# Local attention: per-head exponentials on ScalarE that take the maximum as bias and accumulate the denominators

## What is computed

```python
def local_attention(q, k, v):
    b, h, n, d = q.shape                       # 2, 8, 1024, 64
    w = n // WINDOW                            # windows of 64
    bq = q.reshape(b, h, w, WINDOW, d) * QK_SCALE
    ...
    bk, bv = (look_around(bk), look_around(bv))          # the window before and this one
    ...
    sim = jnp.einsum('bhwid,bhwjd->bhwij', bq, bk)
    mask = (i < j) | (i > j + WINDOW) | (j == -1)
    sim = jnp.where(mask, -jnp.finfo(sim.dtype).max, sim)
    attn = jax.nn.softmax(sim, axis=-1)
    out = jnp.einsum('bhwij,bhwjd->bhwid', attn, bv)
    return out.reshape(b, h, n, d)
```

## Time and profile before

| | us |
|---|---|
| median of 3 runs | 1153.07 (1151.7 to 1158.17) |
| the profiled execution | 1154.28 |
| its span, first to last instruction | 1152.5 |
| mean granted TensorE clock | 0.973 of full |

### The profile page before, as it was taken

One profiled execution on the slowest core, in us unless ns is written; L12 is line 12 of the kernel. 1 busy time (PEld: TensorE's weight loads), 2 busy tenths in 40 slices (PEclk: granted clock), 3 DMA queues, 4 the chain that ended last, 5 costly groups with the idle time before them and its releaser, 6 DMA issues. The chain is left out here.

```text
span 1152.5 us, 22995 instructions
## 1 busy us (share of the span) xinstructions
PE 1072.7 (93%) x8352; PEld 666.0 (58%) x8352; DVE 828.5 (72%) x1522; ACT 633.2 (55%) x1000; POOL 750.5 (65%) x511
## 2 busy tenths in 40 slices
PE   6884899999999999999999999779999898999988
PEld 4552455455454554445545555747777695777677
DVE  6994666666666666666666663579998689888867
ACT  2442356666665565655656564036666455666554
POOL 3662465767677676867667778389986337666526
PEclk8996799999999999999999999889999999999999
DMA  8899621533315243142242100101111100111111
GB/s 257 270 267 354 159 48 48 110 75 83 75 47 111 52 87 89 49 102 59 60 100 65 48 11 20 56 10 31 33 37 37 26 2 15 36 32 33 33 26 36
DMA packets 83456, 89.03 MB, mean 77 GB/s; under 512 B 32740, under 2 KB 66064, under 8 KB 83344
## 3 DMA queue, kind: packets, MB, share of 16 engines
q1 hardware_dynamic: 83344, 87.55, 29.5%
HBM read 53.57 MB, written 24.25 MB: 68 GB/s over the span
## 5 line engine op out<-in xcount | busy, mean ns | idle before, releaser
L863 DVE CUSTOM_DVE_ANT_0 junk<-psum,alibi 128x1024 bf16<-128x1024 f32 x256 | 313.2, 1223 | 205.1 <-PE psum L918 196.8
L834 ACT ACTIVATE E<-psum,keybias_sb 128x1024 f32<-128x1024 f32 x256 | 274.9, 1113 | 234.7 <-PE psum L942 221.4
L767 POOL TENSOR_TENSOR sum_p<-sum_p,E 128x1024 f32<-128x1024 f32 x96 | 232.4, 2421 | 96.2 <-ACT E L834 91.8
L954 PE MATMUL psum<-E,V 128*64 128x512 f32 x1024 | 248.7, 606 | 0.0
L918 PE MATMUL psum<-KH,QH 64*128 64x512 f32 x512 | 118.6, 459 | 12.0 <-PEq L275 6.9
L954 PEld LDWEIGHTS psum<-E,V 128*64 128x64 f32 x1024 | 62.2, 136 | 112.2 <-issue 98.3
L773 POOL TENSOR_TENSOR sum_p<-sum_p,xpos_sb 128x1024 f32<-128x1024 f32 x32 | 76.2, 2382 | 69.0 <-DVE xpos_sb L873 69.0
L918 PEld LDWEIGHTS psum<-KH,QH 64*128 64x128 f32 x512 | 49.4, 189 | 121.5 <-DVE M L863 84.6
L942 PE MATMUL psum<-QH,KH 64*128 64x512 f32 x512 | 102.8, 397 | 5.9 <-DMA QM<-mrow 3.9
L942 PE MATMUL psum<-QL,KH 64*128 64x512 f32 x512 | 101.6, 392 | 0.0
L942 PE MATMUL psum<-QH,KL 64*128 64x512 f32 x512 | 101.4, 392 | 0.0
(11 more groups left out here) (148 smaller groups left out, 2072.5 us busy)
## 6 DMA issues: line engine op xcount, KB each, us to landing
QH<-qa_scratch SPq DMA_DIRECT2D x64, 256.0 KB, 4.2
qa_scratch<-tH SPq DMA_DIRECT2D x8, 1024.0 KB, 5.6
qa_scratch<-tL SPq DMA_DIRECT2D x8, 1024.0 KB, 7.9
QL<-qa_scratch SPq DMA_DIRECT2D x64, 128.0 KB, 4.2
XF<-inverse_scratch SPq DMA_DIRECT2D x32, 256.0 KB, 3.4
vp_att<-v_att SPq DMA_DIRECT2D x64, 128.0 KB, 2.3
KH<-k_scratch SPq DMA_DIRECT2D x16, 256.0 KB, 4.0
KL<-k_scratch SPq DMA_DIRECT2D x16, 256.0 KB, 5.3
```

Of the source, the lines that this page charges most:

```text
L767: pool.tensor_tensor(sum_p[:, s, :], first, E[:, k % 4, :], ALU.add)\
L834: act.activation(E[:, k % 4, :], scores(k % 2), ACT.Exp, bias=kb).then_inc(exp_done, 1)
L863: dve.tensor_tensor_reduce(junk[:, :], banks(max_bank(i, k), 2), alibi[:, s, :], -1.0, BIG, ALU.add, ALU.min, M[:, s, k:k + 1]).then_inc(m ...
L954: last = pe.matmul(banks(6 + i % 2)[HD * ch:HD * ch + HD, :], V[:, g, k, :], E[:, k % 4, ch * 512:(ch + 1) * 512], start=(k == 0), stop=(k ...
```

## The change

`shift_scores` is gone, and `ident_r` with it. `exponentials` becomes eight ACTIVATEs, one per head, of 128 columns each; the bias is that head's column of `nmax` (the negated maximum, now in fp32), and each also writes the sum of its 128 results into its column of `den`. It waits for the maxima. Each of the eight counts on `exp_done`, so all waits for it are in eighths of a tile. `turn_e` waits for four exponentials ahead of the first four transposes and for the other four ahead of the last four. `denominators` keeps the reciprocal alone.

```diff
-    nmax = sb("nmax_att", [P, 2, FH], F32R)
+    nmax = sb("nmax_att", [P, 2, FH])
...
         def exponentials(t, s):
-            need(act, shifted, t + 1)
+            need(act, max_done, t + 1)
             need(act, e_turned, 2 * (t - 1))
-            need(act, den_done, t - 1)
-            act.activation(E[:, s].rearrange("p h c -> p (h c)"), banks(5, 2), ACT.Exp).then_inc(exp_done, 1)
+            need(act, inv_done, t - 1)
+            for n in range(FH):
+                act.activation(E[:, s, n, :], banks(5, 2)[:, n * P:(n + 1) * P], ACT.Exp,
+                               bias=nmax[:, s, n:n + 1],
+                               accum_out=den[:, s, n:n + 1]).then_inc(exp_done, 1)
...
         def maxima(t, s):
             need(dve, scores_done, t + 1)
-            need(dve, shifted, t - 1)
+            need(dve, exp_done, FH * (t - 1))
...
         def denominators(t, s):
-            need(dve, exp_done, t + 1)
-            need(dve, inv_done, t - 1)
-            dve.tensor_reduce(den[:, s, :], E[:, s, :, :], AX_X, ALU.add).then_inc(den_done, 1)
-            need(dve, den_done, t + 1)
+            need(dve, exp_done, FH * (t + 1))
             need(dve, o_done, t - 1)
             dve.reciprocal(den_inv[:, s, :], den[:, s, :]).then_inc(inv_done, 1)
...
         def multiply_qk(t, s):
             need(pe, qkT_done, 2 * (t + 1))
-            need(pe, exp_done, t)
+            need(pe, exp_done, FH * t)
...
-        def shift_scores(t, s):
-
-            need(pe, max_done, t + 1)
-            for n in range(2):
-                last = pe.matmul(banks(5 + n).rearrange("p (h c) -> p h c", c=P), ident_r[:, :],
-                                 nmax[:, s, 4 * n:4 * n + 4][:, :, None].to_broadcast([P, FH // 2, P]),
-                                 start=False, stop=True, skip_group_check=True)
-            last.then_inc(shifted, 1)
-
...
         def turn_e(t, s):
-            need(pe, exp_done, t + 1)
             need(pe, qkT_done, 2 * (t + 1))
             need(pe, eT_done, 2 * t)
             for n in range(2):
+                need(pe, exp_done, FH * t + 4 * (n + 1))
                 for j in range(4):
                     last = pe.transpose(banks(3 + n)[:, j * P:(j + 1) * P], E[:, s, 4 * n + j, :], ident[:, :])
                 last.then_inc(e_turned, 1)
```

More of the change, by code:

```diff
@@ L1023, in adaln_block @@
         ident_w = fsb("ident_w", [P, 2, WIN], BF16)
-        ident_r = fsb("ident_r", [P, P], F32R)
         XS = fsb("XS", [P, T, D // 2])
@@ L1076, in _ @@
                 dve.tensor_copy(ident_b[:, :], ident[:, :])
-                dve.tensor_copy(ident_r[:, :], ident[:, :])
                 for w in range(2):
@@ L1085, in adaln_block @@
             att_sems, attention = local_attention(l, psum, sb, new_sem, dict(before), XF, XA, XS, ident, minus_half,
-                                                  fw_qkv, fw_o, xpos[:, l], mask, mask_b, ident_b, ident_w, ident_r)
+                                                  fw_qkv, fw_o, xpos[:, l], mask, mask_b, ident_b, ident_w)
             before.update(att_sems)
@@ L1122, in local_attention @@
 def local_attention(l, psum, sb, new_sem, before, XF, XA, XS, ident, minus_half, fw_qkv, fw_o, xpos, mask, mask_b,
-                    ident_b, ident_w, ident_r):
+                    ident_b, ident_w):
     def banks(a, n=1):
@@ L1172, in local_attention @@
     max_done = sem("max_done")
-    shifted = sem("shifted")
     exp_done = sem("exp_done")
-    den_done = sem("den_done")
     inv_done = sem("inv_done")
@@ L1476, in project_out @@
             last.then_inc(out_proj, 1)
-        return [(multiply_qk, SCORES), (multiply_v, PV), (project_v, SCORES), (shift_scores, SCORES),
+        return [(multiply_qk, SCORES), (multiply_v, PV), (project_v, SCORES),
                 (project_qk, PROJECT), (turn_e, SCORES), (turn_o, PV), (turn_qk, TURN_QK), (project_out, OUT),
@@ L1624, in turn_x @@
                 pe.wait_ge(before["eT_done"], 2 * T)
-                pe.wait_ge(before["exp_done"], T)
+                pe.wait_ge(before["exp_done"], FH * T)
             pe.transpose(ps_x(s), xn[:, s, :], ident[:, :]).then_inc(x_turned, 1)
```

## The result

The changed kernel takes 1201.6 us (median of 6 runs, 1201.24 to 1205.79) against 1153.48 us (6 runs, 1151.7 to 1158.17): a ratio of 1.0422, 95% interval 1.0397 to 1.0447. It is slower by 48 us, on the forecast side, and inside the range; the forecast was 1194.

A forecast was written before the change was run, and what follows sets the result against it. TensorE, full in steady local-attention steps, was taken as the bound; eight slower exponentials would add 31.2 us in covered and 9.2 in uncovered steps, +40.4 on the profiled 1154.3, median 1.2 lower: 1194 us, range 1168 to 1220.

The forecast's parts named there:

- What bounds the kernel: Local-attention steady steps: TensorE full, 8.98 us without a gap, exponentials hidden; in a layer's last three steps ScalarE's chain shows.
- (1): TensorE loses shift_scores: 0.43 us in each of 26 covered steps, nothing in the 6 uncovered ones.
- (2): VectorE loses the sum of E, 1.21 us a step; not in the chain, so costed at nothing.
- (3): On ScalarE the exponentials start no earlier than behind v's copy, 0.53 us after v's end; waiting on the maxima costs nothing.
- (4): ScalarE's one exponential of 1.018 us becomes eight, start-to-start pitch 0.36 us, between 0.26 and 0.46.
- the second rival: The accumulator's read on ScalarE doesn't overlap at all, pitch about 0.46 or above: 1219 us, or 1232; chance 0.18.
- (5): TensorE's turn_e ends 1.34 us plus eight pitches behind v's end, set by its second half; ScalarE's copies don't bind.
- The same 5.96 us: TensorE's unchanged work behind turn_e in a covered step, from turn_o to the next v projection: 5.96 us.
- The sum: Covered steps +1.20 us (26, +31.2), uncovered +1.54 (6, +9.2): together +40.4 us, forecast 1194 us.
- the rival on the clock: TensorE's clock falls because it pauses every step; a tenth of both stages at half speed gives 1208 us; chance 0.03.
- 1.34 + 8p: Time in us from v's end to turn_e's end, p being the exponentials' start-to-start pitch on ScalarE; 4.22 when uncovered.

The follow-up runs named there:

- e2: Changed kernel with shift_scores back, so no pointer as bias; eight exponentials still write the accumulator: 1167.22 us, ratio 1.0112 to the kernel before.
- e7: Changed kernel with VectorE's sum of E done as well, into a tile that nothing reads: 1197.28 us.
- e9: Changed kernel with the exponentials ahead of v's copy on ScalarE and without the accumulator, VectorE summing E again: 1141.71 us, ratio 0.9896 to the kernel before.
- e1: Changed kernel without the accumulator output, VectorE's sum of E put back: 1175.18 us, ratio 1.0177 to the kernel before.
- e5: Changed kernel with four matmuls of unread results ahead of turn_e in each layer's last three steps: 1191.56 us, ratio 1.0330 to the kernel before.
- e6: Changed kernel with turn_e waiting for all eight exponentials ahead of its first transpose: 1232.75 us, ratio 1.0692 to the kernel before.

## Why the prediction was right, point by point

**What bounds the kernel**: right. TensorE was full, v's copy and the exponential stood hidden beside project_qk with 0.6 us to spare, and the change drew them out.

**(1), (2) what the removed work is worth**: right. shift_scores put back costs nothing (e2), VectorE's sum put back costs nothing in the steps (e7). That the removed matmuls are worth 0.43 us a step once nothing else holds TensorE shows in e9.

**(3) the exponentials start behind v's copy**: right in kind, off by 0.1. They start 0.64 behind v's end in covered steps, not 0.53. The trace gives 0.58 of issue there against 0.45 in uncovered steps; e1, with the pointer, has 0.58 too, while e2, without it, has 0.45. So the pointer belongs to it; why it doesn't show in the uncovered steps stays open.

**(4) the pitch**: taken 0.36 between 0.26 and 0.46, measured 0.344. The nearest rows did this: the Gelus' 0.26 (e1: 0.251) and 0.10 for the read (0.091). The estimate from the Trainium skill, 0.294 us before the accumulator (ScalarE: Activation LUTs, What ACT_TABLE_LOAD costs), is 0.04 too high here. The duration behind it, 280 + 107 = 387 ns, agrees with the rows (mean 379 ns after, 384 in e1), and so do the 93 ns for a pointer (379 after, 286 in e2). Its overlap of 93 ns doesn't: in e1 it is 384 - 251 = 133 ns, and that is the 0.04. The accumulator is read out by an instruction of its own, as the Trainium skill says for VectorE (VectorE: DVE Perf Modes, Two Vector instructions with no wait between them). Both the forecast and the second rival had built on that; the rival's price did not come, since the read overlaps.

**(5) turn_e's second half rules**: right. 0.04 and 0.66 in the chain for 0.04 and 0.67. That ScalarE's copies would not bind was right too: the chain in the steady part never goes over kT. From v's end to turn_e's end a covered step takes 4.26 us for 4.22: here luck had a hand, as the later start (3) and the shorter pitch (4) cancel. "The same 5.96 us" behind it were 5.85, because turn_qk took 0.91 and not 1.03. So the covered step came out at 10.11 for 10.18 (+1.13 for +1.20). The uncovered one, 9.86 us, is +1.31 for +1.54: 0.12 again in turn_qk, 0.10 in the way to turn_e's end, 4.12 for 4.22.

**The sum**: 37.3 us from the steps, 40.4 forecast. The time was 7.6 us above the forecast all the same, and the step that failed is the rival on the clock: "The new step has 8.55 of work in 10.18, 16.8 of 20, in pauses of well under 1 us each, so I expect 1.00." This looked at the covered steps alone. There it holds, but for the first step of layer 1. In the six uncovered ones the chain that I wrote down myself (1.34 + 8p - 0.67 = 3.5 us from v's end to the second half) leaves TensorE with four transposes in 3.5 us, and there the clock fell, in five of six in the trace. e5 puts its price at 10 us. I had priced a tenth of the stages at 14 us and given it a chance of 0.03. The two errors have opposite signs, steps 3.1 us too dear and a clock left out, so the forecast is nearer to the measured time than its treatment of the clock deserves.

## What to carry to other kernels

An accumulator and a pointer as bias are free only in what they take off other engines: on ScalarE each adds about 0.09 us of pitch, so on tiles of 128 columns (0.17 us) the two double the cost. Before work moves to an engine with time to spare, ask where in that engine's order it lands and what waits behind it: the same instructions one place earlier gave 50 us back. And look at the steps at the end of a pipeline apart, where the filler is gone: a longer wait there can be paid twice, the second time as TensorE's clock (here 7.9 us in the uncovered steps, and some 10 by the clock).

## What the runs showed that I had not expected

- The granted clock fell to the lower level behind five of six waits of some 3.5 us in which TensorE did four transposes and nothing else (910 to 930 us after: 0.81), and behind one wait with project_qk in it, the first of layer 1. A fall costs 0.8 us each in turn_qk and project_out and 0.4 each in turn_e's second half and turn_o. Four added matmuls that compute nothing of use brought 10 us (e5).
- Where turn_e waits for all eight exponentials the clock fell in some of the covered steps as well, though project_qk runs ahead of the wait (e6, 12.2 to 12.4 us against 10.73).
- The row of an accumulator read is 0.22 us long and costs 0.09.
- ScalarE's rows grow along a run of neighbours: the eight exponentials go from 0.36 to 0.40 us and the reads from 0.19 to 0.24 within a step, at an even pitch of 0.34. The length of a row is no measure of its cost there; the pitch is.
